# The order of a fused two-layer kernel's preamble: loads, first normalisation, keys and weight splits

## The chip, the cores and the metric

The kernel runs on one core of a Trainium2 chip. The metric is device time in microseconds of one execution.

## The reference

x has 8 sequences of 1024 tokens with 128 features. Two layers each add an attention and a mixture of eight experts to it.

```python
xn = layernorm(x)
x = x + attn0(xn) + ffn0(xn)     # latent attention, 8 heads, keys and values from 32 latents; top-2 of 8 experts
xn = layernorm(x)
x = x + attn1(xn) + ffn1(xn)     # flow attention, linear in the tokens; top-4 of 8 experts
# attn0: q, k = concat(content 128, position 32); softmax(q @ k.T / sqrt(160)) @ v @ W_O
# ffn0: silu(x @ gate.T) * (x @ up.T) @ down.T;  ffn1: (up + 1) * gate * sigmoid(1.702 * gate), clipped
```

## The kernel before

Each engine has a program written out by hand, and the engines meet by semaphores (`x.wait_ge(signal.sem, n)`, `.then_inc`). Every engine works through its own program in order; SP issues all DMAs outside POOL's gathers, on one queue. After a preamble, the programs loop over the eight sequences. In a pass, attention of layer 0 runs tile by tile (`scores`, `neg_max`, exponential, transpose, values), the chosen experts of layer 0 over 23 blocks, the second half of the heads, and then the experts of layer 1 over 32 units with the flow attention beside them. During the units the keys and queries of the next sequence are made. For the first sequence the preamble makes them.

The preamble, engine by engine:

- SP (line 490): x of the first sequence (491), `gate_up1` and `gate_up0` of 2 MB each into `w_raw` (494), then 29 smaller loads (496 to 503), zeroed rows to `x_rows` (507), three stores of the split weights to `w_parts` (511), their completion, four chunks back to `w_split` (520), then `spread_queries` (527, 530), `store_beta` (535) and `load_beta` (539).
- ACT (698 to 702): rounds `gate_up1` in three pieces and `gate_up0` to fp32r (`w_prep`, `w_res`), scales `w_down`; then `copy_xT` (707), `key_base_first` (727), `queries_round` (738), `beta_round` (733), the stores' completion, and `head_round` (744) for four heads.
- DVE (889 to 925): subtracts the rounded parts to get the low ones, sets constants, waits for all loads, clears `w_absorb`, `w_beta` and `query_b`, waits for TensorE's products and copies or scales them to `w_absorb`, `w_beta`, `w_kq`, `w_o`, `b_o`. Then the statistics of x (942 to 949), `norm_apply` (954), `take_latents` (990), `key_base_second` (961), `queries_rest` (974), `beta_rest` (967), the stores' completion, a memset of `key_low` (1012) and `head_rest` (983).
- POOL: constants, a memset of `probs` (626), `rstd` (631); it waits for the last preparation step and adds `b_o` to x in each pass (641).
- TensorE: waits for all loads, makes the absorbed weights (1439, 1440), the transpose of `dq_T` (1442), `w_o` (1445) and `b_o` (1449), waits for the last preparation step of DVE and ACT, then transposes the tokens (1458), makes latents (1487), router logits (1496), the key projection (1467), beta (1476) and the keys of four heads (1480). `scores` (1681) begins the pass.

`PREP_ALL` counts the preparation steps on `prep_sb`. Tiles share memory: `w_prep` lies in `shared`, which later holds the rounded keys, and in `key_low`; `w_raw[1]` in `ffn`; `w_raw[0]` and the small weights in `probsT`. PSUM has eight banks; beta and half of the projection both use bank 6.

## Time and profile before

| | us |
|---|---|
| median of three runs | 2625.56 |
| the three runs | 2624.78, 2625.56, 2633.12 |
| the profiled execution | 2632.35 |
| its span | 2630.6 |

| engine | busy us | share of the span |
|---|---|---|
| TensorE matmul | 2324.5 | 88% |
| DVE | 2083.3 | 79% |
| ACT | 1600.8 | 61% |
| POOL | 712.1 | 27% |

The span is that of one profiled execution, and the busy shares are means over all of it. The preamble is some 3% of the span, so these shares say little about it; timelines and windows of its stretch do. A number in brackets behind a row of a timeline is the idle time of the engine ahead of it, and what ended it. Times in the timelines count from the span's start.

### The profile page before, as it was taken

To read this page: it belongs to the slowest core of one execution; us is meant where nothing else is said; L and a number is where in the kernel's file an instruction comes from. 1 tells how busy PE (TensorE), PEld (TensorE's weight loads), DVE (VectorE), ACT (ScalarE), POOL (GpSimd) and SP (SyncE) were. 2 spreads that over 40 slices of the span, in tenths; PEclk is the share of its full clock that TensorE was granted. 3 is DMA by queue.
4 is the path that set the end of the run, shared out by engine and by line. 5 is a ranking of instruction groups with operands and counts; after the bars stand their busy time and mean duration, and the time that the engine had idled before them with its cause. 6 is when DMAs were issued, how large, how long until landed. Compare 5 with 4: busy or idle time off the path is not lost.

```text
span 2630.6 us, 65321 instructions
## 1 busy us (share of the span) xinstructions
PE 2324.5 (88%) x25647; PEld 1684.5 (64%) x25647; DVE 2083.3 (79%) x3616; ACT 1600.8 (61%) x2891; POOL 712.1 (27%) x601
## 2 busy tenths in 40 slices
PE   3888998899888998889988899898998889988998
PEld 2566766676566755667566676566765666656665
DVE  3869779698796887878877888878788787786976
ACT  2658457574575655766557655667556674575845
POOL 1202342113422043220522215222152122520234
PEclk8899999999999999999999999899999999989989
DMA  6110221102211022110311112111121112211022
GB/s 233 32 44 26 73 66 53 33 15 89 60 48 36 7 93 62 42 41 3 117 38 42 41 42 81 34 50 33 53 80 33 44 30 73 67 34 48 18 73 65
DMA packets 97063, 141.38 MB, mean 54 GB/s; under 512 B 11507, under 2 KB 56508, under 8 KB 96252
## 3 DMA queue, kind: packets, MB, share of 16 engines
q1 hardware_dynamic: 88572, 120.41, 14.7%
q0 software_dynamic: 8192, 16.79, 2.2%
q8 instruction: 211, 3.46, 0.6%
q14 instruction: 88, 0.72, 0.1%
HBM read 101.84 MB, written 31.13 MB: 51 GB/s over the span
## 4 chain that ended last, share of the span: by engine, by line
PE 50%; DVE 26%; issue 15%; ACT 7%; POOL 0%; DVEq 0%; ACTq 0%; POOLq 0%
PE ps L1523 10%; DVE neg_max L1173 10%; PE ps L1530 6%; PE ps L1605 5%; DVE probsT L1183 5%; ACT probs L788 4%; PE ps L1681 4%; PE ps L1718 3%; PE ps L1627 3%; PE ps L1703 2%; PE ps L1480 2%; DVE ffn L1313 2%; PE ps L1544 2%; PE ps L1496 2%; DVE key_low L983 2%
## 5 line engine op out<-in xcount | busy, mean ns | idle before, releaser
L788 ACT ACTIVATE probs<-ps,neg_max 128x1024 f32<-128x1024 f32 x512 | 571.1, 1116 | 181.1 <-DVE neg_max L1173 173.3
L1173 DVE TENSOR_REDUCE neg_max<-ps 128x1 f32<-128x1024 f32 x512 | 620.3, 1213 | 37.9 <-PE ps L1681 29.6
L1523 PE MATMUL ps<-shared,w_split 128*128 128x512 f32 x1536 | 467.1, 441 | 18.7 <-ACT ffn L839 11.7
L1703 PEld LDWEIGHTS ps<-ident,probs 64*128 64x128 f32 x8192 | 339.2, 146 | 120.8 <-issue 72.9
L673 POOL TENSOR_TENSOR probs<-ffn,shared 128x512 f32<-128x512 f32 x208 | 287.9, 1384 | 420.0 <-DVE ffn L1313 166.5
L1523 PEld LDWEIGHTS ps<-shared,w_split 128*128 128x128 f32 x1536 | 286.6, 192 | 166.0 <-issue 63.0
L1703 PE MATMUL ps<-ident,probs 64*128 64x64 f32 x8192 | 359.5, 230 | 19.0 <-ACT probs L788 11.1
L1718 PE MATMUL ps<-probsT,latent 128*32 128x128 f32 x8192 | 331.4, 281 | 50.5 <-DVE o_latent L1166 49.7
L1681 PE MATMUL ps<-shared,query_a 64*128 64x512 f32 x1024 | 271.0, 525 | 112.1 <-ACT probs L788 94.7
L1183 DVE COPY probsT<-ps 128x512 f32<-128x512 f32 x512 | 347.6, 679 | 19.8 <-PE ps L1703 17.9
L839 ACT ACTIVATE ffn<-ps,room_of_gate 128x512 f32<-128x512 f32 x256 | 175.1, 684 | 269.1 <-PE ps L1523 269.1
L772 ACT COPY probsT<-ps 128x512 f32<-128x512 f32 x512 | 296.0, 578 | 30.2 <-PE ps L1703 29.6
L1718 PEld LDWEIGHTS ps<-probsT,latent 128*32 128x32 f32 x8192 | 198.4, 110 | 94.6 <-issue 67.2
L631 POOL TENSOR_TENSOR rstd<-var_eps,minus_half 128x8 f32<-128x8 f32 (+2 forms) x25 | 33.0, 1319 | 834.8 <-DVE var_eps L949 834.8
L1681 PEld LDWEIGHTS ps<-shared,query_a 64*128 64x128 f32 x1024 | 101.9, 195 | 225.4 <-ACT probs L788 179.8
L1681 PE MATMUL ps<-key_low,query_b 64*128 64x512 f32 x1024 | 216.6, 419 | 0.0
L1530 PE MATMUL ps<-probs,w_down 128*128 128x512 f32 x416 | 210.7, 593 | 1.0 <-POOL probs L673 1.0
L1605 PE MATMUL ps<-w_res,shared 128*128 x552 | 183.1, 440 | 17.1 <-DVE ffn L1264 6.8
L852 ACT ACTIVATE ffn<-ffn,silu_bias 128x512 f32<-128x512 f32 x256 | 184.9, 722 | 7.8
L1300 DVE TENSOR_SCALAR ffn<-ps,b_up 128x512 f32<-128x512 f32 x176 | 131.4, 747 | 53.9 <-PE ps L1523 51.4
L1313 DVE SCALAR_TENSOR_TENSOR ffn<-ffn 128x512 f32<-128x512 f32 x176 | 159.6, 907 | 16.1 <-issue 16.1
L1264 DVE TENSOR_TENSOR ffn<-ffn,ps 128x256 f32<-128x256 f32 x184 | 76.5, 419 | 111.4 <-ACT ffn L814 97.8
(231 smaller groups left out, 3443.9 us busy)
## 6 DMA issues: line engine op xcount, KB each, us to landing
w_split<-w_parts SPq DMA_DIRECT2D x132, 256.0 KB, 2.6
shared<-gate_rows SPq DMA_DIRECT2D x64, 512.0 KB, 4.3
y_rows<-probs SPq DMA_DIRECT2D x40, 256.0 KB, 2.2
x_in<-in_x SPq DMA_DIRECT2D x9, 512.0 KB, 4.1
out<-x_mid SPq DMA_DIRECT2D x8, 512.0 KB, 3.2
ffn<-in_gate_up SPq DMA_DIRECT2D x1, 2048.0 KB, 8.5
probsT<-in_gate_up SPq DMA_DIRECT2D x1, 2048.0 KB, 12.7
w_down<-in_down SPq DMA_DIRECT2D x2, 1024.0 KB
```

The costliest lines, as they stand in the source:

```text
L673: nc.gpsimd.tensor_tensor(ffn_h[u % 5], ffn_gu[:, u % 3, :], gate_bc[:, e % GATE_SLOTS, c * BANK:(c + 1) * BANK], ALU.mult).then_inc(h_rea ...
L772: nc.scalar.copy(half_of(t, 0), half_turned(t, 0)).then_inc(low_copied.sem, 1)
L788: nc.scalar.activation(probs[:, t % 3, :], banks(2 * (t % 2)), ACT.Exp, bias=neg_max[:, t % 4:t % 4 + 1], accum_out=row_sum[:, g % 2, t % ...
L1173: nc.vector.tensor_reduce(neg_max[:, t % 4:t % 4 + 1], banks(2 * (t % 2)), X, ALU.max, negate=True).then_inc(max_ready.sem, 1)
L1183: nc.vector.tensor_copy(half_of(t, 1), half_turned(t, 1)).then_inc(high_copied.sem, 1)
L1313: nc.vector.scalar_tensor_tensor(ffn_gu[:, u % 3, :], ffn_u[u % 3], 1.0 - LIMIT, ffn_s[:, u % 3, :], ALU.max, ALU.mult).then_inc(gu_done.s ...
L1523: mm = nc.tensor.matmul(ps[:, bank, :], w_split[:, f % CHUNK_SLOTS, h, k * P:(k + 1) * P], tokens[:, half], start=(part == 0), stop=(part ...
L1530: nc.tensor.matmul(ps[:, 4 + c, :], w_down[1][:, f, :], ffn_h[u % 5], start=False, stop=(f == E * FH - 1)).then_inc(down_done.sem, 1)
L1605: mm = nc.tensor.matmul(ps[:, j % 2, :], xs_parts[x][:, at], w_res_flat[:, bass.ds(first[j] * 4 + h * 2 * F, 2 * F)], start=(part == 0), s ...
L1681: mm = nc.tensor.matmul(ps[:, 2 * (t % 2) + c, :], q[rows, n * P:(n + 1) * P], k[rows, :], start=(part == 0), stop=(part == 1))
L1703: mm = nc.tensor.transpose(ps[:, turn_bank(t, c), k * HQ:(k + 1) * HQ], probs[rows, t % 3, k * P:(k + 1) * P], ident[rows, rows])
L1718: nc.tensor.matmul(ps[DC * j:DC * (j + 1), 7, 0:P], latent[:, k, :], probsT[:, (g % 2) * QUAD + j, k * P:(k + 1) * P], start=(k == 0), sto ...
```

## The change

The preamble is put in another order, on every engine.

- Loads come in two bunches with a semaphore each. After x come the 14 loads that the absorbed weights, the projections and the biases of the first tokens need (`first_in`), then the two of 2 MB, then the zeroed rows, then the others (`weights_in`).
- TensorE waits for `first_in` alone, transposes `dq_T` first, makes the absorbed weights, and goes on to the tokens. The products for `w_o` and `b_o` follow the keys of the four heads, in banks 0 and 1. Beta uses bank 4 in the preamble and comes ahead of the queries' remainder. The wait for all preparation steps follows the keys.
- DVE clears `w_absorb` and `w_beta`, normalises the first tokens, makes `w_kq`, splits `gate_up1` in two pieces, then the absorbed weights, keys, beta, queries and heads, and after them `take_latents`, the split of `gate_up0`, the constants, `w_o` and `b_o`.
- ACT rounds `gate_up1` in two pieces, copies the transposed tokens, rounds `gate_up0`, goes on to the keys; `w_down` is scaled last.
- POOL clears `query_b` ahead of `rstd`, and `probs` and `key_low` behind it.
- The rounded part of `gate_up1` lies in the last two thirds of `shared` (`w_high`), the low part replaces `w_raw[1]`, which moves by 2 * SEQ in `ffn`. Neither covers the keys of the first four heads. The parts are stored in four DMAs, behind `store_beta`, `spread_queries` and `load_beta`; their completion and the four chunk loads come behind that, and ACT and DVE no longer wait for it.

The diff, cut to what the text speaks of (DVE's helpers move up with their bodies unchanged, but that `beta_rest`, `beta_round` and `beta_products` take the bank):

```diff
-PREP_FIRST = 2 + NT + BLOCKS
-PREP_ALL = PREP_FIRST + 5 + 6 + 5
+PREP_ALL = 2 + 1 + 1 + NT + BLOCKS + 3
...
-        w_prep = [v.rearrange("p (f h c) -> p f h c", h=2, c=2 * P)
-                  for v in (shared[:, 0:4 * SEQ], shared[:, 4 * SEQ:6 * SEQ], key_low[:, :, :].rearrange("p h c -> p (h c)"))]
-        W_PIECES = (slice(0, 8), slice(8, 12), slice(12, 16))
+        W_PIECES = (slice(0, CHUNKS // 2), slice(CHUNKS // 2, CHUNKS))
...
-        w_raw = [v.rearrange("p (f c) -> p f c", c=2 * P) for v in (room[:, 4 * SEQ:8 * SEQ], ffn_flat[:, 0:4 * SEQ])]
+        w_raw = [v.rearrange("p (f c) -> p f c", c=2 * P) for v in (room[:, 4 * SEQ:8 * SEQ], ffn_flat[:, 2 * SEQ:6 * SEQ])]
+        w_high = shared[:, 2 * SEQ:6 * SEQ].rearrange("p (f c) -> p f c", c=2 * P)
...
+        first_loads = [
+            (uq_T, "UQ_T"), (uk_T, "UK_T"), (q_rope, "Q_rope"), (dq_T, "DQ_T"), (b_k[:, :], "b_K"),
+            (w_dkv[:, :], "W_DKV"), (w_router[0][:, :], "router0"),
+        ]
         loads = [
-            (uq_T, "UQ_T"), (uk_T, "UK_T"), (uv_T, "UV_T"), (wo_heads, "W_O"), (b_uv, "b_UV"), (dq_T, "DQ_T"),
-            (q_rope, "Q_rope"), (b_k[:, :], "b_K"), (w_dkv[:, :], "W_DKV"),
-            (w_down[0][:, :, :], "down0"),
-            (w_router[0][:, :], "router0"), (w_qkv[:, :], "W_QKV"), (w_proj[:, :], "W_PROJ"),
-            (w_down[1][:, :, :], "down1"),
+            (uv_T, "UV_T"), (wo_heads, "W_O"), (b_uv, "b_UV"), (w_down[0][:, :, :], "down0"),
+            (w_qkv[:, :], "W_QKV"), (w_proj[:, :], "W_PROJ"), (w_down[1][:, :, :], "down1"),
             (w_router[1][:, :], "router1"), (b_gate[:, :], "b_gate"), (b_up[:, :], "b_up"), (b_down[:, :], "b_down"),
         ]
-        rows = [(b_dkv, "b_DKV", DC), (b_o_in, "b_O", D), (b_qkv, "b_QKV", 3 * D), (b_proj, "b_PROJ", D),
-                (b_router, "b_ROUTER", E)]
-        ALL_WEIGHTS = 16 * (len(loads) + len(rows) + QUAD + HALVES)
+        rows = [(b_o_in, "b_O", D), (b_qkv, "b_QKV", 3 * D), (b_proj, "b_PROJ", D), (b_router, "b_ROUTER", E)]
+        FIRST_WEIGHTS = 16 * (len(first_loads) + 1 + QUAD + HALVES)
+        ALL_WEIGHTS = 16 * (len(loads) + len(rows))
...
+            for dst, name in first_loads:
+                sp.dma_start(dst, ins[name]).then_inc(first_in.sem, 16)
+            for c in range(HALVES):
+                sp.dma_start(w_kq[:, c, KD * c:KD * (c + 1)], ins["W_K"][:, 0:KD]).then_inc(first_in.sem, 16)
+            for j in range(QUAD):
+                sp.dma_start(b_dq[DC * j:DC * (j + 1), :], ins["b_DQ1"][0:DC, :]).then_inc(first_in.sem, 16)
+            sp.dma_start(b_dkv[:, :], ins["b_DKV"].partition_broadcast(P)).then_inc(first_in.sem, 16)
...
                 sp.dma_start(w_raw[l], ins[f"gate_up{l}"].rearrange("p f a b -> p f (a b)")).then_inc(raw_in[l].sem, 16)
...
+            sp.wait_ge(rows_zeroed.sem, 1)
+            sp.dma_start(x_rows[:, :].rearrange("(j p) d -> p j d", p=P), ys).then_inc(rows_zeroed.sem, 16)
             for dst, name in loads:
                 sp.dma_start(dst, ins[name]).then_inc(weights_in.sem, 16)
             for dst, name, n in rows:

                 sp.dma_start(dst[:, 0:n], ins[name].partition_broadcast(P)).then_inc(weights_in.sem, 16)
             sp.sem_inc(y_stored.sem, 1)
-
-            sp.wait_ge(rows_zeroed.sem, 1)
-            sp.dma_start(x_rows[:, :].rearrange("(j p) d -> p j d", p=P), ys).then_inc(rows_zeroed.sem, 16)
...
-            for i, piece in enumerate(W_PIECES):
-                sp.wait_ge(prep_low.sem, i + 1)
-                sp.dma_start(w_parts[piece, :, :].rearrange("f p c -> p f c"),
-                             w_prep[i].rearrange("p f h c -> p f (h c)").bitcast(F32)
-                             ).then_inc(parts_stored[i].sem, 16)
-            for stored in parts_stored:
-                sp.wait_ge(stored.sem, 16)
...
-            for f in range(CHUNK_SLOTS):
-                load_chunk(f)
+            store_beta(None)
             spread_queries(None)
-            store_beta(None)
             sp.wait_ge(low_zeroed.sem, 1)
             sp.wait_ge(beta_stored.sem, beta_stored.at(None, 16))
             load_beta(0)
+
+            for i, piece in enumerate(W_PIECES):
+                sp.wait_ge(prep_low.sem, i + 1)
+                for h, part in enumerate((w_high[:, piece, :].bitcast(F32), w_raw[1][:, piece, :])):
+                    sp.dma_start(w_parts[piece, :, h * 2 * P:(h + 1) * 2 * P].rearrange("f p c -> p f c"),
+                                 part).then_inc(parts_stored[i].sem, 16)
+            for stored in parts_stored:
+                sp.wait_ge(stored.sem, 32)
+            for f in range(CHUNK_SLOTS):
+                load_chunk(f)
...
-            nc.gpsimd.memset(probs[:, :, :], 0.0).then_inc(rows_zeroed.sem, 1)
+            nc.gpsimd.memset(query_b[:, :].bitcast(F32), 0.0).then_inc(query_zeroed.sem, 1)
+            pool.wait_ge(query_zeroed.sem, 1)
+            for c in range(2):
+                nc.gpsimd.memset(query_b[2 * DC * c + DC:2 * DC * c + DC + 2, :].bitcast(F32), 1.0
+                                 ).then_inc(query_zeroed.sem, 1)
+                pool.wait_ge(query_zeroed.sem, 2 + c)
...
             inverse_deviation(None, 1)
+            nc.gpsimd.memset(probs[:, :, :], 0.0).then_inc(rows_zeroed.sem, 1)
+            nc.gpsimd.memset(key_low[:, :, :].bitcast(F32), 0.0).then_inc(low_zeroed.sem, 1)
             pool.wait_ge(prep_sb.sem, PREP_ALL)
...
             act.wait_ge(raw_in[1].sem, 16)
             for i, piece in enumerate(W_PIECES):
-                nc.scalar.copy(w_prep[i][:, :, 0, :], w_raw[1][:, piece, :]).then_inc(prep_high.sem, 1)
-            act.wait_ge(raw_in[0].sem, 16)
-            nc.scalar.copy(w_res[:, :, 0, :], w_raw[0].rearrange("p (e a) c -> p e (a c)", e=E)).then_inc(res_high.sem, 1)
-            act.wait_ge(weights_in.sem, ALL_WEIGHTS)
-            nc.scalar.mul(w_down[1][:, :, :], w_down[1][:, :, :], 1.0 / ALPHA).then_inc(prep_act.sem, 1)
+                nc.scalar.copy(w_high[:, piece, :], w_raw[1][:, piece, :]).then_inc(prep_high.sem, 1)
...
             copy_xT(None, 0, 0, 6)
+            act.wait_ge(raw_in[0].sem, 16)
+            nc.scalar.copy(w_res[:, :, 0, :], w_raw[0].rearrange("p (e a) c -> p e (a c)", e=E)).then_inc(res_high.sem, 1)
             key_base_first(None)
+            beta_round(None, 4)
             queries_round(None)
-            beta_round(None)
-            for stored in parts_stored:
-
-                act.wait_ge(stored.sem, 16)
             for h in range(QUAD):
                 head_round(None, h, RUN_BANKS[h], h + 1)
+            act.wait_ge(weights_in.sem, ALL_WEIGHTS)
+            nc.scalar.mul(w_down[1][:, :, :], w_down[1][:, :, :], 1.0 / ALPHA).then_inc(prep_act.sem, 1)
             act.wait_ge(rows_zeroed.sem, 17)
             act.wait_ge(limits_ready.sem, 2)
...
+            nc.vector.memset(w_absorb[:, :, :], 0.0).then_inc(prep_sb.sem, 1)
+            nc.vector.memset(w_beta[:, :], 0.0).then_inc(prep_sb.sem, 1)
...
+            nc.vector.memset(spare[:, 1:2], 0.0).then_inc(y_added.sem, 1)
+            dve.wait_ge(x_loaded.sem, 16)
+            link(norm_stats(x_in, range(NT)), aggregates_next=True)
+            norm_variance()
+            dve.wait_ge(rstd_ready.sem, 1)
+            norm_apply(0, x_in, range(NT))
+            dve.wait_ge(prep_mm.sem, 1)
+            for c in range(HALVES):
+                nc.vector.tensor_copy(w_kq[:, c, KD * (1 - c):KD * (2 - c)].rearrange("p (a b) -> p a b", a=2),
+                                      ps[:, 1, 0:DC].unsqueeze(1).to_broadcast([P, 2, DC])).then_inc(kq_ready.sem, 1)
             for i, piece in enumerate(W_PIECES):
                 dve.wait_ge(prep_high.sem, i + 1)
-                nc.vector.tensor_tensor(w_prep[i][:, :, 1, :], w_raw[1][:, piece, :],
-                                        w_prep[i][:, :, 0, :].bitcast(F32), ALU.subtract).then_inc(prep_low.sem, 1)
+                nc.vector.tensor_tensor(w_raw[1][:, piece, :].bitcast(F32R), w_raw[1][:, piece, :],
+                                        w_high[:, piece, :].bitcast(F32), ALU.subtract).then_inc(prep_low.sem, 1)
+            dve.wait_ge(prep_sb.sem, 2)
+            dve.wait_ge(prep_mm.sem, 2)
+            for c, rows in enumerate(STRIPS):
+                made = ps[rows, 0, 0:H0 * (DC + 1)].rearrange("p (h i) -> p h i", h=H0)
+                nc.vector.tensor_scalar(w_beta[rows, H0 * c:H0 * (c + 1)], made[:, :, DC], SCALE, None, ALU.mult
+                                        ).then_inc(absorb_ready.sem, 1)
+                for copy in range(2):
+                    at = KD * c + DC * copy
+                    nc.vector.tensor_scalar(w_absorb[rows, :, at:at + DC], made[:, :, 0:DC], SCALE, None, ALU.mult
+                                            ).then_inc(absorb_ready.sem, 1)
+            key_base_second()
+            beta_rest(4)
+            for c in range(2):
+                queries_rest(c)
+            dve.wait_ge(low_zeroed.sem, 1)
+            for h in range(QUAD):
+                head_rest(h, RUN_BANKS[h], h + 1)
+            take_latents(None, 5)
+            assert count[0] == DVE_STEPS_BEFORE, count[0]
             dve.wait_ge(res_high.sem, 1)
             nc.vector.tensor_tensor(w_res[:, :, 1, :], w_raw[0].rearrange("p (e a) c -> p e (a c)", e=E),
                                     w_res[:, :, 0, :].bitcast(F32), ALU.subtract).then_inc(prep_sb.sem, 1)
...
-            nc.vector.tensor_copy(w_o[:, :, :].rearrange("p a b -> p (a b)"), ps[:, 4, 0:QUADS * D]
+            nc.vector.tensor_scalar(b_up[:, :], b_up[:, :], 1.0, None, ALU.add).then_inc(prep_sb.sem, 1)
+            dve.wait_ge(prep_mm.sem, 3)
+            nc.vector.tensor_copy(w_o[:, :, :].rearrange("p a b -> p (a b)"), ps[:, 0, 0:QUADS * D]
                                   ).then_inc(prep_sb.sem, 1)
-            nc.vector.tensor_tensor(b_o[:, :], ps[:, 5, 0:D], b_o_in, ALU.add).then_inc(prep_sb.sem, 1)
-
...
-            take_latents(None, 5)
-            key_base_second()
-            for c in range(2):
-                queries_rest(c)
-            beta_rest()
-            assert count[0] == DVE_STEPS_BEFORE, count[0]
-            for stored in parts_stored:
-
-                dve.wait_ge(stored.sem, 16)
-            nc.vector.memset(key_low[:, :, :].bitcast(F32), 0.0).then_inc(low_zeroed.sem, 1)
-            dve.wait_ge(low_zeroed.sem, 1)
-            for h in range(QUAD):
-                head_rest(h, RUN_BANKS[h], h + 1)
...
-            pe.wait_ge(weights_in.sem, ALL_WEIGHTS)
+            pe.wait_ge(first_in.sem, FIRST_WEIGHTS)
             pe.wait_ge(pool_consts.sem, 11)
-
+            nc.tensor.transpose(ps[:, 1, 0:DC], dq_T, ident[0:DC, 0:DC]).then_inc(prep_mm.sem, 1)
...
-            nc.tensor.transpose(ps[:, 1, 0:DC], dq_T, ident[0:DC, 0:DC])
-            for h in range(H0):
-
-                nc.tensor.matmul(ps[DC * (h % QUAD):DC * (h % QUAD + 1), 4, (h // QUAD) * D:(h // QUAD + 1) * D],
-                                 uv_T[:, h, :], wo_heads[:, h, :], start=True, stop=True)
-            for h in range(H0):
-
-                mm = nc.tensor.matmul(ps[:, 5, 0:D], b_uv[:, h:h + 1].to_broadcast([P, P]), wo_heads[:, h, :],
-                                      start=(h == 0), stop=(h == H0 - 1))
+                    mm = nc.tensor.matmul(ps[KD * c + DC:KD * (c + 1), 0, at], q_rope[:, h, :],
+                                          ident[0:DC + 1, 0:DC + 1], start=True, stop=True)
             mm.then_inc(prep_mm.sem, 1)
-            pe.wait_ge(prep_sb.sem, PREP_ALL)
-            pe.wait_ge(prep_act.sem, 1)
...
+                if bank == 6:
+                    pe.wait_ge(query_low.sem, query_low.at(b, 2))
+                nc.tensor.matmul(ps[0:2 * H0, bank, :], w_beta[:, :], key_base, start=True, stop=True
...
             router(None, 0, 5, NT * DC)
+            pe.wait_ge(kq_ready.sem, HALVES)
             key_projection(None)
-            beta_products(None)
-            pe.wait_ge(beta_ready.sem, beta_ready.at(None, 1))
+            pe.wait_ge(absorb_ready.sem, 6)
+            beta_products(None, 4)
+            pe.wait_ge(query_low.sem, query_low.at(None, 2))
             for h in range(QUAD):
                 head_keys(h, RUN_BANKS[h])
+            pe.wait_ge(weights_in.sem, ALL_WEIGHTS)
+            for h in range(H0):
+
+                nc.tensor.matmul(ps[DC * (h % QUAD):DC * (h % QUAD + 1), 0, (h // QUAD) * D:(h // QUAD + 1) * D],
+                                 uv_T[:, h, :], wo_heads[:, h, :], start=True, stop=True)
+            for h in range(H0):
+
+                mm = nc.tensor.matmul(ps[:, 1, 0:D], b_uv[:, h:h + 1].to_broadcast([P, P]), wo_heads[:, h, :],
+                                      start=(h == 0), stop=(h == H0 - 1))
+            mm.then_inc(prep_mm.sem, 1)
+            pe.wait_ge(prep_sb.sem, PREP_ALL)
+            pe.wait_ge(prep_act.sem, 1)
```

## Rows read from the trace of the kernel before

**Rows 1.** The chain that ended last, 0 to 110 us: start us, us, what
```profile
6.01 39.67 issue
...
77.94 1.24 DVE neg_max L1173
```
**Rows 2.** Who waited for whom, 0 to 80 us: us in total, times, longest
```profile
PE ps L1439 <- DMA b_router<-in_b_ROUTER: 27.4, 1, 27.4
```
**Rows 3.** SP's timeline: start us, us, engine, line, what it issues, count
```profile
3.33 1.82 SPq L498 DMA_DIRECT2D b_dq<-in_b_DQ  x4
...
7.08 2.66 SPq L500 DMA_DIRECT2D probsT<-in_b_UV  x1
...
22.61 7.22 SPq L511 DMA_DIRECT2D w_parts<-shared  x2
...
137.08 0.80 SPq L559 DMA_DIRECT2D ffn<-x_rows  x1
```
**Rows 4.** Timeline of TensorE (PEld loads weights) and DVE, 27 to 43 us
```profile
27.41 0.32 PE L1439 MATMUL ps<-probsT 128*32 128x33 f32 x2 [27.41 <-DMA b_router<-in_b_ROUTER]
...
36.55 3.49 PEld L1449 LDWEIGHTS ps<-probsT 128*128 128x128 f32 x16 [0.38 <-issue]
...
42.38 0.41 DVE L921 COPY w_o<-ps 128x256 f32<-128x256 f32 x1
```
**Rows 5.** The same timeline, 49 to 64 us
```profile
49.93 2.18 PE L1458 MATMUL ps<-ident,x_norm_first 128*128 128x128 f32 x8 [9.59 <-DVE x_norm_first L954]
...
52.78 3.49 PEld L1487 LDWEIGHTS ps<-w_dkv,xT_first 128*128 128x128 f32 x16 [0.97 <-ACT xT_first L707]
...
63.43 0.76 DVE L961 TENSOR_SCALAR xT_first<-ps,b_k 64x512 f32<-64x512 f32 x1 [3.06 <-PE ps L1467]
```
**Rows 6.** The same timeline, 66 to 80 us
```profile
66.54 1.02 PE L1476 MATMUL ps<-xT_first,w_beta 128*16 128x512 f32 x2 [3.14 <-DVE query_a L974]
...
68.93 6.39 PE L1480 MATMUL ps<-xT_first,w_absorb 128*128 128x512 f32 x8 [1.38 <-DVE o_latent L967]
...
75.08 2.83 DVE L983 TENSOR_TENSOR key_low<-ps,shared 32x512 fp32r<-32x512 f32 x4 [0.31 <-ACT shared L744]
...
78.05 0.79 PE L1681 MATMUL ps<-shared,query_a 64*128 64x512 f32 x2 [2.07 <-DVE key_low L983]
...
79.44 1.22 DVE L1173 TENSOR_REDUCE neg_max<-ps 128x1 f32<-128x1024 f32 x1
```
**Rows 7.** DMA issues, 0 to 100 us: KB each, median us to landing
```profile
ffn<-in_gate_up SPq DMA_DIRECT2D x1, 2048.0 KB, 8.5
...
x_in<-in_x SPq DMA_DIRECT2D x2, 512.0 KB, 4.0
...
beta_rows<-o_latent SPq DMA_DIRECT2D x1, 64.0 KB, 2.1
```
**Rows 8.** Windows: us, busy us (and count) per engine, granted clock, DMA, GB/s
```profile
10.00:20.00 10.00, 0.00 (x0) 0.00 (x0) 6.26 (x4) 7.20 (x4) 0.00 (x0) 1.00 0.91 333
...
36.00:39.00 3.00, 3.00 (x23) 2.62 (x16) 0.00 (x0) 0.00 (x0) 0.00 (x0) 1.00 1.05 409
54.00:57.00 3.00, 3.00 (x16) 3.00 (x15) 0.00 (x0) 0.00 (x0) 0.00 (x0) 0.50 0.00 0
...
74.00:76.00 2.00, 1.98 (x7) 0.57 (x5) 1.63 (x4) 1.18 (x2) 0.00 (x0) 0.91 0.75 210
```
**Rows 9.** Timeline of POOL, ACT and DVE, 3 to 23 us
```profile
3.35 2.66 POOL L626 MEMSET probs<- 128x3072 f32 x1
...
9.80 2.85 ACT L698 CAST shared<-ffn 128x2048 fp32r<-128x2048 f32 x2 [7.74 <-DMA ffn<-in_gate_up]
...
11.73 3.43 DVE L889 TENSOR_TENSOR shared<-ffn,shared 128x2048 fp32r<-128x2048 f32 x2 [11.73 <-ACT shared L698]
...
18.30 4.42 DVE L892 TENSOR_TENSOR w_res<-probsT,w_res 128x4096 fp32r<-128x4096 f32 x1 [2.00 <-ACT w_res L700]
```
**Rows 10.** Line 954, 40 to 60 us: ns min/median/max, first and last start
```profile
L954 DVE TENSOR_SCALAR x_norm_first<-x_in,mean_var,rstd x8: 334/338/2357, 47.4 to 51.2; 128x128 f32<-128x128 f32 x8
```

77 lines of the change are left out of this document (29 added, 48 removed).

## Prediction

> **What bounds the kernel now.** I began with the chain of waits over the first 110 us and the list of who waited for whom before 80 us. In [rows 1] the reader is to see how little the chain knows of the start: 39.67 us of it are "issue". The list of waits fills that stretch: TensorE stood 27.4 us for the last small load [rows 2]. Then I read the timeline engine by engine. The program has a preamble of 75 to 78 us and eight passes over a sequence. The change rewrites the preamble alone; in the passes only a bank number becomes an argument, with the same value. So what is needed is when the first `neg_max` of pass 0 starts, 77.94 us now [rows 1], and whether the passes follow that shift one to one.
>
> The preamble is one serial chain with three parts. To 27.4 us everything waits for the DMAs: SP issues 2 MB twice ahead of the small loads, and TensorE's first wait is for all of them [rows 2, 3]. From 27.41 to 40.3 us TensorE multiplies weights [rows 4]. Only then, DVE being in order and its program putting these results first, come normalisation (43.11 to 51.57), transposes, latents, router, key projection (to 63.43), queries, the keys of four heads (to 77.91), and attention [rows 5, 6]. The profile has the first tokens in SBUF at 0.79 + 4.0 = 4.8 us [rows 7], 38 us before DVE touches them.
>
> **The clock in the preamble.** This decides each TensorE term, so it is settled first. The windows say 1.00 at 36 to 39 us and 0.50 at 54 to 57 us [rows 8]. Yet sixteen 128x128 weight loads took 3.49 us at 36.55 (granted 1.00) and 3.49 us at 52.78 (granted 0.50) [rows 4, 5]. So the pace was that of 0.50 (1.2 GHz) in both, and I use the durations as they stand. The row at 74 to 76 us (0.91, [rows 8]) is the first in which it rose for working matmuls; ahead of it lay the dense 512-column matmuls from 68.93 on [rows 6]. The Trainium skill ("TensorE: Matmul & The Clock Gate", Part 1, the caveats under "Seeing it yourself") warns that recorded clock events on this chip are unreliable; the equal 3.49 us agrees with that.
>
> **The change, part by part.**
>
> *Loads in two bunches.* After x, SP issues 14 small DMAs before the two large ones. Such issues now take about 0.47 us each from one start to the next (four `b_dq` in 1.82, [rows 3]), so the last starts at 1.28 + 13 x 0.47 = 7.4 us. A DMA of 64 KB took 2.1 us to land [rows 7]: first bunch in at 9.5 us, say 9.8. The bound above: now b_UV and DQ_T held SP for 2.66 and 1.82 us behind 4 MB (the first in [rows 3]); nothing large is ahead of them in the new order, but one such hold would give 12.5. Below, 9.3. The Trainium skill ("DMA: Bandwidth & Descriptors", Specifications) asks for 512 B or more per transfer and says smaller ones become read-modify-writes. By it this bunch, whose bias, router and W_K rows are all smaller, could land later than bytes suggest. No row prices it alone; it is rival C.
>
> *Large loads.* Issued at 7.9 and 8.4 instead of 1.28 and 1.90. Now raw1 was in at 9.80 and raw0 at 14.66, each 4.9 us of transfer (the first by [rows 7, 9]); flow begins a little over 1 us after issue, so raw1 at 14.6 and raw0 at 19.5.
>
> *First tokens at once.* DVE takes statistics at 4.9; from 43.11 to the end of `rstd` (47.39) were 4.3 us, so 9.2. POOL's zeroing of `query_b` is at most 3 x 0.9 after 3.4 us and is over. Applying took 4.15 us, of which the first tile took 2357 ns against 338 of the others, beside POOL's 2.35 us `x_mid` [rows 10]. So a POOL instruction can hold such a DVE instruction for its whole length. In the new order POOL zeroes `probs` (2.66 us for 3072 columns, [rows 9]) and `key_low` (2048 columns, so 1.8) just then. Held by both: 9.2 + 2.7 + 1.8 + 8 x 0.34 = 16.4 us; held by neither 11.9. Either way ahead of 18.0, next paragraph, so it costs nothing.
>
> *Products.* 32 matmul pairs at 0.247 us each, 27.41 to 35.3 (the first in [rows 4]), plus one transpose of 0.31: 9.8 to 18.0 us. The output products (35.54 to 40.33, 4.8 us) move behind the keys.
>
> *Weight splits between.* ACT copies halves of 128x2048: 14.6 to 16.5 to 18.4 (2.85 us took 3072 columns, [rows 9]). DVE subtracts to 21.1 (3.43 us for 3072 columns, so 2.3 each, [rows 9]), then scales absorb and beta, 1.7 us (40.37 to 42.08): 22.8. ACT is free at 18.4, and its first copy of xT is due at 19.1. Cover: 0.7 us on ACT; if raw1 is x us later than 15.3, the chain is x later.
>
> *Transposes to key projection.* Transposes to second copy of xT took 49.93 to 52.73 = 2.8 us; latents, router and projection 52.78 to 63.43 = 10.7 [rows 5]. 18.0 + 2.8 + 10.7 = 31.5 us; call it T. It was 63.43. The 3.6 us copy of `w_res` on ACT (20.9 to 24.5) lies beside.
>
> *Beta before the queries.* TensorE no longer waits for `query_low` before beta. T + 0.76 (key base), + 1.1 (beta product), + 0.57 (ACT), + 0.68 (DVE), then two query remainders of 0.77: T + 4.7 to head keys, against 68.93, T + 5.5, now [rows 5, 6]. Head keys to the last `key_low`: 68.93 to 77.91 = 9.0 [rows 6]. DVE is free at 31.5 + 4.7 + 9.0 = 45.2 us.
>
> *What now stands between keys and attention.* TensorE, POOL and DVE still wait for the last preparation step, and that tail moved behind the keys on DVE: latents 0.55, split of `w_res` 4.42 [rows 9], memsets 0.8, two small scalings 0.34, `w_o` and `b_o` 0.61 [rows 4]. Sum 6.7: 51.9, and with semaphores 52.2 us. TensorE's own tail: heads end at 36.2 + 6.4 = 42.6, output products 4.8 to 47.4; DVE needs them at 51.3, so 3.9 us of cover. ACT's `w_down` (1.91 us) ends near 45. First scores at 52.2; from scores to a `neg_max` at this clock 79.44 - 78.05 = 1.4 [rows 6]: 53.6 us. POOL's `x_mid` now falls beside that reduction instead of beside the norm: 0 to 2.35 us. The nearest row is the held first tile, but that was SBUF to SBUF and this reads PSUM, so I take 0 and keep 2.35.
>
> *DMA queue.* All loads but the first bunch, with the zeroed x_rows, are 8.9 MB from about 9.5 us. At the 333 GB/s of 10 to 20 us [rows 8] they end at 36. TensorE needs the last at 42.6, DVE's tail from 46.5 on. SP passes from them to the beta store (34.7), six query DMAs of 0.6 each from 36.2, and the beta loads at about 40; in by 42.5, not late. The 4.2 MB of stores, four DMAs at most 18.7 us in all (22.61 to 41.3 now, the first of them in [rows 3], a backlog included), and the four chunk loads follow, behind which stands the reload of x and, far later, the load of xs at 137.08 now [rows 3]. They cost nothing; that is rival D.
>
> Sum: 77.94 - 53.6 = 24.3 us. The profiled execution took 2632.35 (span 2630.6), which gives 2608.0. It lies 6.8 above the median, though, and the three timed runs (2624.78, 2625.56, 2633.12) hold both levels. On the median the forecast is 2625.56 - 24.3 = 2601.3.
>
> **The rivals.**
>
> *A, as summed: 2601.* For it: the serial chain and unchanged durations. Chance 0.62.
>
> *B, TensorE runs at full speed in the preparation.* From 9.8 to 31.5 us it hardly pauses, where now it pauses from 40.3 to 49.9. The Trainium skill (the same page, Part 1, "The two states you'll see") says sustained work brings 2.4 GHz; by it this stretch would be warm. In rows: sixteen 128-row transposes and products at half their time save up to 5.3 of 10.7 us, and head keys would be bound by DVE (8 x 0.69) for another 1.4. That is 6.7 more: 2595. Against it: 13.5 us of nearly unbroken work from 49.93 to 63.4 ran wholly at 0.50 (54 to 57 us of it in [rows 8]). Chance 0.14.
>
> *C, the DMAs become the bound.* The first bunch in at 12.5 instead of 9.8 moves all by 2.7; raw1 after 15.3 holds ACT's copy of xT; or the last load comes after 46.5, from which point DVE waits for the output products. With 8.9 MB at 250 GB/s that would be 45, at 220 50. Prices 3 to 8 us, so 2604 to 2609; `x_mid` holding DVE belongs here, 2603.7. The same bounds hold for DVE's tail being slower. Chance 0.19.
>
> *D, slower: the deferred stores hold SP.* SP waits for all four in its own order before anything of pass 0. The load of xs is due at 137.08 - 24.3 = 112.8 us, 72 us after the stores are issued. At half-row pieces, twice 18.7 us is 37. From 72 us on they would delay the pass, and from 96 us (4.2 MB at 44 GB/s) the kernel would be slower than now; say 2630. The rate was 409 GB/s while they ran at 36 to 39 us [rows 8]. Chance 0.02.
>
> *E, the gain isn't passed on.* If pass 0 were held by something at a fixed time, or the loops ran slower, the result would be within 8 us of 2625. I find none: x is reloaded and all weights are in by 60 us. Chance 0.03.
>
> **How the numbers follow.** 2601.3 is A. B and C with the two levels of the runs before give 2591 to 2612; beyond lie D, E and both bounds at once. Three tenths of a per cent, 7.9 us, is about what a measurement of this kernel can tell from no change. Faster 0.95 (A, B, C), same 0.03 (E), slower 0.02 (D).
>
> **What would show it.** In the changed profile: TensorE's first matmul at about 10 us; the key projection ends near 31.5 (27 would be B, 35 C); last `key_low` at 45; the `w_res` subtraction at 46 with TensorE already done with the output products; first `neg_max` at 53.6. The stores of `w_parts` lie at 40 to 60 us beside attention. The forecast fails if that first reduction stands elsewhere, or if the span shrinks by another amount than it moved.

## The result, and the profile after

The changed kernel took 2604.01 us, the median of 6 runs (2599.76 to 2611.58). The kernel before took 2626.36 on the same chip (6 runs, 2623.89 to 2633.12). The ratio is 0.991, with a 95% interval of 0.9896 to 0.9924. The forecast was 2601.3 within 2591 to 2612. The profiled execution took 2604.15 (span 2602.4), against 2632.35 (span 2630.6) before.

The views are those read before. First the chain of waits of the changed kernel, 0 to 60 us (start us, us, what):

```profile
7.44 0.42 SPq L502
7.90 8.97 DMA ffn<-in_gate_up
16.90 3.70 ACT shared L710 x2
20.60 1.06 ACT xT_first L715 x2
21.71 3.62 PE ps L1479 x16
25.33 3.37 PE ps L1488 x16
28.70 3.63 PE ps L1458 x4
32.35 0.77 DVE xT_first L931
...
47.28 4.33 DVE w_res L1001
...
54.44 1.24 DVE neg_max L1175
```

The 39.67 us of "issue" of [rows 1] are gone, and the long pieces now have an owner. The first `neg_max` starts at 54.44 instead of 77.94. The new start of the chain isn't the small loads, but the 2 MB load behind them and ACT's two copies of it. The timeline of the changed kernel tells how much that is worth (start us, us, engine, line, what; in brackets the idle time ahead and what ended it):

```profile
9.30 6.00 DVE L924 TENSOR_SCALAR x_norm_first<-x_in,mean_var,rstd 128x128 f32<-128x128 f32 x8 [1.85 <-POOL rstd L641]
10.93 0.31 PE L1436 MATMUL ps<-ident,probsT 32*128 32x32 f32 x1 [10.93 <-DMA b_dkv<-in_b_DKV]
...
12.33 11.41 SPq L508 DMA_DIRECT2D probsT<-in_UV_T  x1
...
16.90 3.70 ACT L710 CAST shared<-ffn 128x2048 fp32r<-128x2048 f32 x2 [14.83 <-DMA ffn<-in_gate_up]
...
19.06 1.97 PE L1449 MATMUL ps<-ident,x_norm_first 128*128 128x128 f32 x8
20.50 1.15 ACT L715 COPY xT_first<-ps 128x512 f32<-128x512 f32 x2
...
21.71 3.62 PE L1479 MATMUL ps<-w_dkv,xT_first 128*128 128x32 f32 x16 [0.68 <-ACT xT_first L715]
```

TensorE starts its products at 10.93, where [rows 4] had 27.41, and the eight transposes follow them with no gap. From their start to the latents are 2.65 us (21.71 - 19.06). In the kernel with the old load order below, where ACT had been free for 22 us, the same stretch took 2.64 (37.44 - 34.80). So ACT was late by next to nothing, though the chain goes through it: two paths arrive together. The next stretch of the same timeline is the keys and the tail:

```profile
33.26 1.86 PE L1468 MATMUL ps<-xT_first,w_beta 128*16 128x512 f32 x2 [0.94 <-DVE xT_first L931]
...
38.07 5.30 PE L1472 MATMUL ps<-xT_first,w_absorb 128*128 128x512 f32 x8 [2.95 <-DVE query_a L944]
...
40.87 5.70 DVE L953 TENSOR_TENSOR key_low<-ps,shared 32x512 fp32r<-32x512 f32 x8 [2.85 <-ACT shared L752]
...
43.88 2.05 PE L1660 MATMUL ps<-probsT 128*128 128x128 f32 x16
...
47.20 4.42 DVE L1001 TENSOR_TENSOR w_res<-probsT,w_res 128x4096 fp32r<-128x4096 f32 x1
...
53.10 0.80 PE L1687 MATMUL ps<-shared,query_a 64*128 64x512 f32 x2 [7.17 <-DVE b_o L1016]
```

TensorE has finished all its preparation at 45.9 us and then stands 7.17 us for `b_o`, which DVE writes last. In between lies one operation that no score reads, the split of `w_res`. The tail on DVE is the last link of the new chain.

Does the run pass the shift on? The first neg_max moved by 23.5 us. The first store of a result moved from 396.81 to 374.23, so by 22.6; the fifth from 1672.99 to 1646.90, by 26.1; the medians by 22.35. Between are the same passes. From one such store to the next were 317.7 to 319.7 us before and 313.2 to 321.0 after, over all eight, so single passes scatter by some us. The span of the two profiled executions shrank by 28.2, which is 4.7 more than the start moved; the last pass alone gave 4.4 of that (313.2 against 317.7), and the one before it had taken 321.0. A single span can't test the shift to such a degree: the changed kernel, profiled again (control below), had a span of 2593.1 instead of 2602.4 with its start only 0.3 us earlier.

### The profile page after: what moved, and what is told of

Same layout as the page of the kernel before. It is cut to its first block, busy times and chain, and to the rows that moved or that the text cites. A ratio compares the mean times of both kernels' runs of the same rounds, so it can differ in the third digit from the quotient of the medians.

```text
span 2602.4 us, 65321 instructions
## 1 busy us (share of the span) xinstructions
PE 2318.3 (89%) x25647; PEld 1679.3 (65%) x25647; DVE 2080.8 (80%) x3611; ACT 1600.3 (61%) x2890; POOL 717.4 (28%) x605
## 4 chain that ended last, share of the span: by engine, by line
PE 52%; DVE 26%; issue 14%; ACT 7%; DMA 0%; SPq 0%; DVEq 0%; POOL 0%; ACTq 0%; POOLq 0%
PE ps L1515 10%; DVE neg_max L1175 10%; PE ps L1522 6%; PE ps L1597 5%; DVE probsT L1185 5%; PE ps L1687 4%; PE ps L1724 4%; ACT probs L797 3%; PE ps L1709 3%; PE ps L1619 3%; PE ps L1472 2%; DVE ffn L1315 2%; PE ps L1536 2%; PE ps L1488 2%; DVE key_low L953 2%
## 6 DMA issues: line engine op xcount, KB each, us to landing
probsT<-in_gate_up SPq DMA_DIRECT2D x1, 2048.0 KB, 14.1
```

## The experiments

The theory is that of the prediction: a serial chain to the keys, whose parts each pass their full length on, and behind it DVE's tail as the new bound. Against it stand, run by run, the loads, SP's order of issue and the clock as the bound.

One number orders the runs: the start of the first `neg_max` in the profiled run. Medians of one program differ by some us from one set of runs to the next (control below), while that start repeated within 0.4 (54.44 and 54.11). It is not exact either: two kernels below with the same instructions up to there differ by 1.6 us, through TensorE's pace. Each time stands beside the kernel before on the same chip; the rows of one chip share its median.

| kernel | first neg_max | earlier than 77.94 by | median us | below before by | ratio (95%) |
|---|---|---|---|---|---|
| changed | 54.44 | 23.5 | 2604.01 | 22.4 | 0.991 (0.9896 to 0.9924) |
| changed, again | 54.11 | 23.8 | 2600.40 | 26.8 | 0.9901 (0.9884 to 0.9919) |
| old load order | 70.23 | 7.7 | 2618.74 | 9.5 | 0.996 (0.9945 to 0.9974) |
| norm first alone | 71.86 | 6.1 | 2619.46 | 8.8 | 0.9968 (0.9955 to 0.998) |
| residual early | 48.43 | 29.5 | 2595.71 | 32.6 | 0.9879 (0.9865 to 0.9894) |
| stores first | 58.12 | 19.8 | 2604.54 | 23.7 | 0.9913 (0.99 to 0.9926) |
| both of these | 57.90 | 20.0 | 2605.18 | 21.5 | 0.9928 (0.9909 to 0.9946) |
| warm first | 53.17 | 24.8 | 2606.06 | 20.6 | 0.9922 (0.99 to 0.9944) |
| keys before latents | 46.98 | 31.0 | 2600.09 | 26.5 | 0.9896 (0.9875 to 0.9918) |
| the same, residual early | 42.55 | 35.4 | 2589.56 | 37.1 | 0.9851 (0.9834 to 0.9868) |
| keys first, tokens apart | 44.11 | 33.8 | 2593.61 | 33.6 | 0.9865 (0.9844 to 0.9885) |
| products at once | 43.89 | 34.1 | 2596.82 | 30.4 | 0.987 (0.9851 to 0.9889) |

The third and fifth columns differ by 4.4 us at most, and by 0.3 on the mean over the twelve. The time follows the shift, one to one as far as rows can tell that scatter by 3 us each (standard deviation).

### What the load order is worth

```diff
+            for l in (1, 0):
+                sp.dma_start(w_raw[l], ins[f"gate_up{l}"].rearrange("p f a b -> p f (a b)")).then_inc(raw_in[l].sem, 16)
             for dst, name in first_loads:
...
             pe.wait_ge(first_in.sem, FIRST_WEIGHTS)
+            pe.wait_ge(weights_in.sem, ALL_WEIGHTS)
```

The large loads go ahead of the small ones again, the store of zeroed x_rows behind all loads, and TensorE waits for every load; the rest of the change stays.

> The changed kernel, with the two 2 MB loads back behind x and ahead of the small ones, the zeroed rows behind all loads, and TensorE waiting for all loads before its first product. Theory 1 (the order of the loads carries most of the gain, the chain behind it is serial): first product at 27 to 28 us instead of 10.9, first neg_max at 70 to 71, about 2620.5. Theory 2 (the gain comes from doing normalisation and splits beside the products, whatever the loads do): the loss is under 8 us, 2612 or less.

Timeline of TensorE in this kernel:

```profile
26.69 0.28 PE L1437 MATMUL ps<-ident,probsT 32*128 32x32 f32 x1 [26.69 <-DMA b_router<-in_b_ROUTER]
```

The first product is 15.8 us later than in the changed kernel (26.69 against 10.93), and so is the first neg_max (70.23 against 54.44). Nothing behind absorbed it. This was forecast (70 to 71). Two thirds of the gain, 15.8 of 23.5 us, are the order of the loads together with TensorE's shorter first wait; the edit moves both, and no run has one without the other.

### Normalising first, in the kernel before

The DVE program of the kernel before, with its weight work moved behind `norm_apply(0, x_in, range(NT))`; loads and all other engines as before.

```diff
-            for i, piece in enumerate(W_PIECES):
-                dve.wait_ge(prep_high.sem, i + 1)
...
             norm_apply(0, x_in, range(NT))
+            for i, piece in enumerate(W_PIECES):
+                dve.wait_ge(prep_high.sem, i + 1)
...
+            dve.wait_ge(prep_sb.sem, PREP_ALL)
```

> The kernel before, with one edit: DVE takes the statistics of the first tokens and normalises them at the start of its program, as soon as x is in. Loads, stores and all else as before. Theory 1: TensorE's transposes start when the last preparation step is done, at about 43.1 instead of 49.9 us, and the rest follows: 6.8 us less, 2619.5 against 2626.4. Theory 2 (the chain has another late input in that place, such as the weight splits on DVE that the normalisation now pushes back, or POOL's memset that holds it): less than 3 us gained.

```profile
9.20 2.14 DVE L912 TENSOR_SCALAR x_norm_first<-x_in,mean_var,rstd 128x128 f32<-128x128 f32 x8 [1.78 <-POOL rstd L631]
```

The first neg_max came 6.1 us earlier, where 6.8 were expected. The transposes started at 43.73 instead of 49.93 [rows 5], right after the weight work. The row shows one thing more: with no POOL instruction beside it the normalisation took 2.14 us, where it takes 6.00 in the changed kernel. So the old load order leaves the change 7.7 of its 23.5 us, and normalising first alone gives 6.1.

### Is DVE's tail the bound

```diff
+            dve.wait_ge(res_high.sem, 1)
+            nc.vector.tensor_tensor(w_res[:, :, 1, :], w_raw[0].rearrange("p (e a) c -> p e (a c)", e=E),
+                                    w_res[:, :, 0, :].bitcast(F32), ALU.subtract).then_inc(prep_sb.sem, 1)
...
             key_base_second()
             beta_rest(4)
...
             take_latents(None, 5)
...
-            dve.wait_ge(res_high.sem, 1)
-            nc.vector.tensor_tensor(w_res[:, :, 1, :], w_raw[0].rearrange("p (e a) c -> p e (a c)", e=E),
```

DVE splits `w_res`, and writes the constants behind it, while it waits for TensorE's latents, router and key projection.

> The changed kernel, with the split of w_res (4.42 us on DVE) and the constants (0.8 us) put ahead of the key base, into the 7.4 us in which DVE waits for the key projection, instead of behind the keys. Theory 1 (DVE's tail behind the keys sets the start of attention): the first neg_max moves from 54.4 to about 49.2 us, and the median from 2604 to about 2599. Theory 2 (something else stands ready only then: TensorE's output products, ACT's w_down, the beta loads or the last load): the first neg_max moves by less than 1.5 us and the time stays at 2603 to 2605.

Timeline of DVE in this kernel:

```profile
25.75 4.43 DVE L992 TENSOR_TENSOR w_res<-probsT,w_res 128x4096 fp32r<-128x4096 f32 x1 [0.99 <-ACT w_res L756]
...
47.25 0.28 DVE L1016 TENSOR_TENSOR b_o<-ps,probsT 128x128 f32<-128x128 f32 x1
48.43 1.23 DVE L1175 TENSOR_REDUCE neg_max<-ps 128x1 f32<-128x1024 f32 x1 [0.90 <-PE ps L1687]
```

`b_o` came at 47.25 instead of 52.76, and the first neg_max 6.0 us earlier (5.2 were expected). The keys ended 0.4 us earlier in this execution, at 46.13 instead of 46.57, so 5.6 are the edit's. The operation costs what it did (4.43 us), and now lies in a gap. The forecast had listed exactly this sum as "what now stands between keys and attention"; it was the bound, and an avoidable one.

### Where the stores stand on SP

```diff
-            store_beta(None)
-            spread_queries(None)
...
-            load_beta(0)
             for i, piece in enumerate(W_PIECES):
...
             for f in range(CHUNK_SLOTS):
                 load_chunk(f)
+            store_beta(None)
+            spread_queries(None)
...
+            load_beta(0)
```

SP stores the weight splits, waits for them, and loads the chunks before the keys' small DMAs. That undoes the part "keys ahead of the stores". It was run on the changed kernel and on the one with the residual early.

> The changed kernel, with the four stores of the split weights, their completion and the four chunk loads put back ahead of SP's beta store, query spreads and beta loads. Theory 1: SP has the stores done at about 44 us, the beta loads land near 52.5 us, still ahead of TensorE's first scores at 53.1; so this part of the change is worth 0 to 1 us here (2604 to 2605), hidden under DVE's tail. Theory 2: the stores in the queue push the keys' DMAs behind attention's start: first scores at 58 or later, 2609 or more.

> The early split of w_res together with the stores, their completion and the chunk loads ahead of SP's beta store, query spreads and beta loads. With the stores first alone the first neg_max stood at 58.1 us, set by the beta loads at 56.8, and not by DVE. Theory 1 (start of attention decides, and the longer of two chains sets it): the first neg_max again at about 57.5 to 58.5 us, 9 to 10 us behind the early split alone, and the time 7 to 10 us above it (2603 to 2605 against 2595.7). Theory 2 (part of a late start is made up within the first pass, as the stores-first run with its 0.5 us for a start 3.7 us later may suggest): 4 us or less above it.

SP's and TensorE's timelines of the second of these:

```profile
32.08 2.63 SPq L543 DMA_DIRECT2D w_parts<-ffn  x1
...
46.71 1.76 SPq L517 DMA_DIRECT2D w_split<-w_parts  x4
48.51 0.43 SPq L532 DMA_DIRECT2D beta_rows<-o_latent  x1
...
54.06 0.56 SPq L536 DMA_DIRECT2D key_low<-beta_rows  x2
...
56.56 0.80 PE L1687 MATMUL ps<-shared,query_a 64*128 64x512 f32 x2 [10.31 <-DMA key_low<-beta_rows]
```

`beta_rows` waits on SP until 48.5, though DVE finishes `o_latent` at about 36.7, and the scores start when the beta rows are back. On the changed kernel this cost 3.7 us of start (58.12), since DVE's tail would have held the scores to 53.1 anyway. My bound for it, a start of the scores no later than 53.1, was wrong. With the tail gone the same edit cost 9.5 us (57.90 against 48.43). The medians, taken on two chips, lie 21.5 and 32.6 below the kernel before on each, which is 11.1 apart. The start is the later of two chains, about 58 by SP and 54.4 or 48.4 by DVE. The 3.7 us alone can't be seen in the medians (2604.54 against 2604.01 and 2600.40); the 9.5 can.

### The clock in the preparation

```diff
+            for i in range(4):
+                nc.tensor.matmul(ps[:, 7, :], ident[:, :], w_absorb[:, 0:4, :].rearrange("p h c -> p (h c)"),
+                                 start=True, stop=True)
             pe.wait_ge(first_in.sem, FIRST_WEIGHTS)
```

Four large matmuls, whose result nobody reads, fill TensorE's wait for the first loads.

> The changed kernel, with four dense 128x512 float32 matmuls (eight passes) of zeros into a PSUM bank that is overwritten later, put on TensorE ahead of its wait for the first loads, where it stood idle to 10.9 us. Theory 1 (mine: the matmuls of 33, 32 and 8 columns do not keep the engine at full speed, so latents, router and key projection run at the half rate whatever comes first): the sixteen latent passes again take 3.6 us, the first neg_max stays at 54 to 55 us, no change beyond 2 us. Theory 2 (the half rate comes from the idle start alone): the latents take about 1.9 us, the key projection ends near 27 instead of 32.3, and the first neg_max comes 5 us earlier.

TensorE's timeline, and two windows of this kernel (window, us, busy us and count of PE, PEld, DVE, ACT, POOL, granted clock, DMA share, GB/s):

```profile
3.45 5.63 PE L1437 MATMUL ps<-w_absorb,ident 128*128 128x512 f32 x8 [3.45 <-POOL before L629]
10.88 0.24 PE L1440 MATMUL ps<-ident,probsT 32*128 32x32 f32 x1 [1.79 <-DMA b_dkv<-in_b_DKV]
...
21.19 3.62 PE L1483 MATMUL ps<-w_dkv,xT_first 128*128 128x32 f32 x16 [1.52 <-ACT xT_first L715]
```

```profile
11.00:16.00 5.00, 5.00 (x52) 3.75 (x52) 4.58 (x10) 0.00 (x0) 2.64 (x2) 0.82 0.97 387
21.00:25.00 4.00, 3.81 (x18) 3.81 (x19) 3.47 (x7) 3.39 (x2) 0.00 (x0) 0.50 1.11 337
```

The clock rose ahead of the products, which took 6.8 us instead of 8.1, and fell in the middle of them: a pair took 0.24 to 0.25 us up to the one at 14.08, and 0.32 from the one at 14.25 on (granted 1.00 at 13 to 14 us, 0.50 from 15 us). TensorE had not paused since 10.88, so the fall wasn't brought by a pause; the 1.52 us ahead of the latents came later. The latents took the same 3.62 us. The transposes started 1.35 earlier, the latents only 0.52: ACT's copies of raw1 were then the later path. The whole gain is 1.3 us of start, 0.9 against the control, too little for the medians. In this run four large matmuls ahead of the small ones didn't keep TensorE fast through them.

### What the latents in the middle cost

Latents and router feed nothing in the scores of the first keys. Here the key projection and beta product go ahead of them, and the router behind the head keys. The key base overwrites the first half of the transposed tokens, so latents and router are computed in part from overwritten tokens in the next two kernels; their operations and sizes are unchanged. Their starts can be read; whether other routing changes the time of their passes isn't shown, so their medians count for less. In the second of them the residual is split in two halves that lie in DVE's gaps around beta.

```diff
             transpose_norm(None, 0, 6)
-            latents(None, 5, range(NT))
-            router(None, 0, 5, NT * DC)
             key_projection(None)
             beta_products(None, 4)
+            latents(None, 5, range(NT))
...
                 head_keys(h, RUN_BANKS[h])
+            router(None, 0, 5, NT * DC)
```

> The changed kernel, with the key projection ahead of latents and router on TensorE, latents behind beta, router behind the head keys. Theory 1 (latents and router, 7.0 us of weight loads, stand on the keys' chain for nothing): the key projection ends at about 25.5 instead of 32.35, and the first neg_max comes 5 to 7 us earlier, 47.5 to 49.5, the head keys being held a little by the latents; about 2598. Theory 2 (TensorE's sum of work, not the order, sets the end: router and output products now end late and hold DVE's tail): less than 3 us.

> Both edits: key projection ahead of latents and router, and the split of w_res in two halves (2.2 us each) in DVE's gaps around beta, the constants ahead of the heads. By the sums TensorE is then the bound: heads to about 38, router and output products to 43 or 44, first scores near 44.5 and first neg_max at 45 to 46, 3 us before the early split alone (48.4); the time 2591 to 2593. The rival: the halves on DVE push the heads' low parts by as much as they save behind them, first neg_max at 48 or later and no gain over the early split alone.

TensorE's timeline of the first:

```profile
27.26 2.46 PE L1479 MATMUL ps<-w_dkv,xT_first 128*128 128x32 f32 x16
...
36.34 1.85 PE L1488 MATMUL ps<-w_router,xT_first 128*128 128x8 f32 x16
```

The key base came 6.9 us earlier (25.41 against 32.35) and the first neg_max 7.5 (46.98). The router's 16 matmuls behind the head keys took 1.85 us instead of 3.56. Part of the 7.5 is pace: the beta product took 1.02 us here and 1.86 in the changed kernel. With the residual in two halves as well, the first neg_max stood at 42.55, 11.9 earlier than in the changed kernel and earlier than the 45 to 46 that was expected.

### Keys first with the tokens kept apart, and the control

```diff
+                    to = o_rest if b is None else xT[l]
-                    nc.scalar.copy(xT[l][:, c * BANK:(c + 1) * BANK], ps[:, bank + c, :]).then_inc(xT_ready.sem, 1)
+                    nc.scalar.copy(to[:, c * BANK:(c + 1) * BANK], ps[:, bank + c, :]).then_inc(xT_ready.sem, 1)
```

The same order with the first sequence's transposed tokens in `o_rest`, free at that time, so that nothing is overwritten; the residual in two halves, as above. Beside it the changed kernel was run again.

> The changed kernel itself again, beside the next two on the same chip. First neg_max at 54.4 us (within 0.5), time 2602 to 2606; it gives what the same program differs by from call to call, and so what half a microsecond between two other kernels is worth.

> The two edits together (key projection ahead of latents and router, the split of w_res in two halves beside beta), with the transpose of the first tokens in o_rest, so that the key base no longer overwrites what latents and router read. The instructions and their order are those of the run before it, so the first neg_max again at 42.5 to 43 us and the time at 2588 to 2592. The rival: the first tokens' copy into other memory costs, or a longer-lived buffer holds a later step; first neg_max at 44 or later.

TensorE's head keys in the kernel before this one (tokens overwritten) and in the new version:

```profile
31.79 4.96 PE L1474 MATMUL ps<-xT_first,w_absorb 128*128 128x512 f32 x8
```

```profile
31.78 6.53 PE L1476 MATMUL ps<-xT_first,w_absorb 128*128 128x512 f32 x8
```

Timeline of DVE in the new version:

```profile
37.91 2.83 DVE L954 TENSOR_TENSOR key_low<-ps,shared 32x512 fp32r<-32x512 f32 x4 [0.31 <-ACT shared L753]
...
42.59 0.42 DVE L1017 COPY w_o<-ps 128x256 f32<-128x256 f32 x1 [0.98 <-PE ps L1666]
```

It took 2593.61 us against 2600.40 of the changed kernel and 2627.19 of the kernel before, on one chip. The start is 10.0 us earlier than the control's; the single runs of the two overlap (2583.02 to 2598.79, and 2593.82 to 2607.75), so of the two differences that of the start is the sure one. The first neg_max is at 44.11, behind the 42.5 to 43 I had worked out and where the rival had it (44 or later). The rival's reason isn't seen, though: the same instructions start the head keys at 31.79 and 31.78 in the two kernels and then take 4.96 and 6.53 us, which is a difference of TensorE's pace. For that reason DVE, done at 41.6, waits 0.98 us for the output products. The control says how exact a median is here: 2600.40 now and 2604.01 before, for the same program.

### What bounds the preamble next

The last kernel adds three things: the first bunch cut down to what the products read, so that they start at once; POOL's memsets behind the normalisation; the splits of gate_up1 behind the key base. DVE's constants go to its start, and the second half of the residual behind the latents.

```diff
-        FIRST_WEIGHTS = 16 * (len(first_loads) + 1 + QUAD + HALVES)
+        FIRST_WEIGHTS = 16 * len(first_loads)
+        SECOND_WEIGHTS = 16 * (len(second_loads) + 1 + QUAD + HALVES)
...
+            pool.wait_ge(norm_ready.sem, NT)
             nc.gpsimd.memset(probs[:, :, :], 0.0).then_inc(rows_zeroed.sem, 1)
```

> The same, and further: TensorE's first wait is for the four loads of the absorbed weights alone (the other ten small ones get a semaphore of their own, waited for ahead of the key projection); POOL zeroes probs and key_low behind the normalisation; ACT and DVE do the transposed tokens and the key base ahead of the rounding of gate_up1. Theory 1 (the last of the small loads, b_dkv, held the first product to 10.9 us, and POOL's memsets held the normalisation for 3.9 us): first product at 5 to 6 us, normalisation 2.2 us long instead of 6.0, key projection ends near 20 us, and the first neg_max at about 40.5 us, where DVE's sum of work and the last loads (33 us, then 3 to 5 us of output products) set the end; time 2 us below the run before it. Theory 2 (that order gains nothing, since the loads set the end): first neg_max within 0.7 us of the run before it.

Timeline of TensorE and DVE in this kernel:

```profile
6.09 0.31 PE L1448 MATMUL ps<-ident,probsT 32*128 32x32 f32 x1 [6.09 <-DMA probsT<-in_DQ_T]
...
38.05 1.08 PE L1672 MATMUL ps<-probsT 128*32 128x128 f32 x16 [6.51 <-DMA b_router<-in_b_ROUTER]
...
42.37 0.42 DVE L1026 COPY w_o<-ps 128x256 f32<-128x256 f32 x1 [2.65 <-PE ps L1676]
```

The products started 4.8 us earlier, the key base was there at 20.75 instead of 25.65, and the keys ended at 36.65. The first neg_max, expected at 40.5, is only 0.2 us earlier. TensorE stood 6.51 us for the last load, which landed at 38 us and not at the 33 I had worked with, and then needed 4.3 for the output products. Those took 2.6 in the version above; while TensorE stood idle the granted clock had fallen (0.71 at 34 to 36 us, 0.50 at 36 to 40), so the wait costs more than its length. From here the loads are the bound, the last of which SP issues at 30.60. In time it can't be told from the version above.

## Why the prediction was right, point by point

The start of the first `neg_max` was forecast at 53.6 and is 54.44. That closeness is partly luck of opposite errors; the terms were:

| term | forecast us | measured us |
|---|---|---|
| first bunch in, products start | 9.8 | 10.93 |
| products | 8.2 | 8.13 |
| transposes to key base (T) | 13.5 | 13.29 |
| T to head keys | 4.7 | 5.72 |
| head keys to last key_low | 9.0 | 8.5 |
| DVE's tail to the scores | 7.0 | 6.53 |
| scores to neg_max | 1.4 | 1.34 |

*Loads.* 1.1 us short. The issues came at the pace forecast: the last of the bunch started at 7.44. Its landing was mis-sized: I took the 2.1 us of a 64 KB DMA [rows 7], and the last small one took 3.5 (7.44 to 10.9). The large ones landed 9.0 and 14.1 us after their issue, raw1 at 16.9 instead of 14.6. There I had taken the 4.9 us between two landings as a transfer and added 1.8 us ahead of it; the whole 8.5 us of [rows 7] would have given 16.4. That is rival C by its place, but hardly by its price: the cover on ACT, 0.7 us and the 1.1 by which the products were late, was used up, and not more. The old order is worth 15.8 us.

*First tokens at once.* The forecast had the normalisation end at 16.4 at the latest; it ended at 15.3, and the products hid it to 19.06. DVE was held, as the bound said: the longest of its eight tiles took 4406 ns, the other rows stayed at 335, and without POOL beside it all eight took 2.14 us.

*Beta before the queries.* T + 5.7 instead of T + 4.7. The beta product took 1.86 us where I had 1.1 from [rows 6] (1.02). Its size isn't fixed: the same program took 1.86 in one execution and 1.02 in the control, and head keys started at 38.07 and 37.27. Nor is that of the next term, 8.5 us here and 9.0 in the control, so only 0.3 of those 0.8 reached the start. Taking a duration at full pace behind a stretch that I had at half pace was the step that failed; both ends belonged into the sum. It came of a wrong reading of the rows: I called the window of 74 to 76 us the first in which the clock rose [rows 8], while the product of 66.54 [rows 6] had run at full pace already, in a window (66 to 67 us) of 1.00. The rest of the 1.0 us is gaps between the steps.

*Tail.* 6.53 against 7.0, and the early residual shows that it was on the path. TensorE's output products took 2.7 us instead of 4.8, so the cover was 6.5 us (done at 45.9, read at 52.4) and not 3.9. POOL's `x_mid` ran beside the first `neg_max` (53.13, 2.38 us) and the reduction took 1.23 as ever: the zero taken there was right, and the 2.35 kept for the range not needed.

*Clock, rival B.* False: latents and router took 3.62 and 3.56, as in [rows 5]. The key base came at 32.35, between A's 31.5 and C's 35.

*Stores, rival D.* False in the place I feared: SP had issued the reload of x at 57.31, and the load of xs stands at 112.55. The stores ran beside attention. The order of stores and beta on SP, to which the sum gave no price of its own, has one: without it the start is 3.7 us later, and 9.5 once DVE's tail is gone.

*Rival E.* False: the twelve rows follow the shift, within 0.3 us on the mean. Of the two signs of failing that I had named, the second did show, the span having shrunk by 4.7 us more than the start moved. It was badly chosen: two spans of the same program lie 9.3 us apart.

*The time.* 24.3 us were forecast from the shift and 23.5 came; the medians give 22.35, and 26.8 in the control. The remaining difference to 2601.3 is inside what a median of this kernel can tell, so the nearness of the number is no proof of the terms; the table above is.

## What to carry to other kernels

In a preamble that runs once, write down when each operand is in memory and when its engine first touches it: here x lay there for 38 us, and the first wait of TensorE was for loads it didn't need. After such a chain has been shortened, look at the program order of the engine that finishes last: here 5.6 us more were one operation of DVE, with the constants behind it, that had to move into a gap 20 us earlier, and some 7 were matmuls whose results the first scores don't read (each measured alone). Where a gain is near the scatter of the medians, measure the start of the first steady step in the profile.
